# Splitting the score and maximum products of an attention stage into two matmuls of 64 weight columns

## What is computed

```
h = 8 heads of size 8, scale = 64 ** -0.5, n = 1056 rows, 8 samples
q, k, v = split(x @ w_qkv + b_qkv)
dots = einsum('bhid,bhjd->bhij', q, k) * scale
attn = softmax(dots, axis=-1)
out  = einsum('bhij,bhjd->bhid', attn, v)
```

## Time and profile before

| | |
|---|---|
| three runs | 2658.01, 2625.93, 2634.01 us; median 2634.01 us |
| profiled execution | 2648.98 us, its span 2647.2 us |
| mean granted TensorE clock | 0.86 of full speed |
| TensorE, VectorE, ScalarE busy | 81%, 50%, 43% of the span |
| attention stage | from 275.6 us (first maximum product) to 1234.8 us (last weighing) |

### The profile page before, as it was taken

One profiled execution on the slowest core, in us unless ns is written; L12 is line 12 of the kernel. 1 busy time (PEld: TensorE's weight loads), 2 busy tenths in 40 slices (PEclk: granted clock), 3 DMA queues, 4 the chain that ended last, 5 costly groups with the idle time before them and its releaser, 6 DMA issues. The chain is left out here.

```text
span 2647.2 us, 40358 instructions
## 1 busy us (share of the span) xinstructions
PE 2134.6 (81%) x14306; PEld 962.7 (36%) x14306; DVE 1323.2 (50%) x3515; ACT 1139.9 (43%) x2082; POOL 210.5 (8%) x238
## 2 busy tenths in 40 slices
PE   8975788888888888886758999970755998599999
PEld 4134122222222222211544544430324996345454
DVE  0036867777677777740124443437876443333331
ACT  0012066666666666664114454430521331254544
POOL 0021000000000000000000000003310133100000
PEclk9976589999899989987558999995876997699999
DMA  6825402121221212001110000000000000000000
GB/s 108 149 80 180 86 21 42 22 44 23 45 39 36 40 27 41 14 10 42 66 57 1 1 1 1 1 2 2 0 0 3 1 2 1 22 5 9 5 9 9
DMA packets 60311, 82.61 MB, mean 31 GB/s; under 512 B 26555, under 2 KB 45396, under 8 KB 57068
## 3 DMA queue, kind: packets, MB, share of 16 engines
q1 hardware_dynamic: 57036, 71.60, 12.6%
q0 software_dynamic: 3104, 8.72, 0.9%
HBM read 53.16 MB, written 27.14 MB: 30 GB/s over the span
## 5 line engine op out<-in xcount | busy, mean ns | idle before, releaser
L532 ACT ACTIVATE b_prob<-b_p_s 128x512 f32<-128x512 f32 x1104 | 590.2, 594 | 361.1 <-PE b_p_s L661 316.8
L546 DVE TENSOR_REDUCE b_m<-b_p_m 128x1 f32<-128x1024 f32 x512 | 602.4, 1219 | 215.7 <-PE b_p_m L608 214.7
L661 PE MATMUL b_p_s<-b_q,b_k 51*128 51x512 bf16 x1024 | 365.5, 420 | 120.1 <-DVE b_m L546 97.3
L608 PE MATMUL b_p_m<-b_k,b_q 48*128 48x512 bf16 x1024 | 374.7, 430 | 46.6 <-DMA b_k<-qk_scr 25.5
L688 PE MATMUL b_p_o<-b_prob,b_v 128*32 128x512 f32 x2304 | 340.9, 667 | 0.0
L661 PEld LDWEIGHTS b_p_s<-b_q,b_k 51*128 51x128 bf16 x1024 | 82.9, 96 | 509.1 <-DVE b_m L546 256.9
L1124 ACT ACTIVATE d_hidden<-d_p_z 128x704 f32<-128x704 f32 x192 | 135.5, 755 | 145.1 <-PE d_p_z L1028 144.8
L1124 ACT ACTIVATE n_hidden<-n_p_z 128x704 f32<-128x704 f32 x192 | 135.2, 755 | 127.8 <-PE n_p_z L1028 127.8
L1242 DVE TENSOR_TENSOR d_xg<-d_xd,d_p_c 128x352 f32<-128x352 f32 x192 | 91.3, 517 | 181.2 <-PE d_p_c L1017 181.2
L1242 DVE TENSOR_TENSOR n_xg<-n_xd,n_p_c 128x352 f32<-128x352 f32 x96 | 49.9, 520 | 203.4 <-PE n_p_c L1017 203.4
L1028 PE MATMUL d_p_z<-d_xg,d_w 64*128 64x352 f32 x768 | 144.0, 494 | 0.0
(11 more groups left out here) (317 smaller groups left out, 2584.2 us busy)
## 6 DMA issues: line engine op xcount, KB each, us to landing
xt<-in_x SPq DMA_DIRECT2D x16, 1024.0 KB, 11.7
v_scr<-a_vw SPq DMA_DIRECT2D x8, 1152.0 KB, 4.8
b_v<-v_scr SPq DMA_DIRECT2D x8, 1152.0 KB, 12.2
c_sums<-sum_scr SPq DMA_DIRECT2D x8, 1056.0 KB, 5.8
sum_scr<-b_sums POOLq DMA_DIRECT2D x32, 256.0 KB, 2.3
qk_scr<-a_qk_part SPq DMA_DIRECT2D x24, 264.0 KB, 2.9
b_q<-qk_scr SPq DMA_DIRECT2D x96, 66.0 KB
b_k<-qk_scr SPq DMA_DIRECT2D x16, 198.0 KB
```

Of the source, the lines that this page charges most:

```text
L532: nc.scalar.activation(prob[:, U % PR_RING, 0:w], p_s[:, U % S_RING, 0:w], ACT.Exp, scale=float(D) ** -0.5).then_inc(exp_done, 1)
L546: nc.vector.tensor_reduce(m3[:, x, 0:1], p_m[:, s, :, :].rearrange("p k n -> p (k n)"), axis=AX.X, op=ALU.max).then_inc(rows_free, 1)
L608: last = nc.tensor.matmul(out[:, k, :], q_st[s][r, i, t * P:t * P + P], k_st[s][r, i, k * WIDE:k * WIDE + WIDE], start=True, stop=True)
L661: last = nc.tensor.matmul(out, k_st[s][r, q, jt * P:jt * P + P], q_st[s][r, q, a * WIDE:a * WIDE + WIDE], start=True, stop=True)
```

## The change

Each of the 64 maximum products and 64 score products of a quad (L608 and L661) becomes two matmuls with 64 weight columns each. The first writes partitions 0 to 63 of the same PSUM bank, the second partitions 64 to 127. Both read the same moving operand. The semaphore is raised by the second. Waits, buffers, the order of the work and every other matmul stay as they are.

```diff
                     if x < FULL_ROWS:
                         i, t = divmod(x, FULL)
                         for k in range(2):
-                            last = nc.tensor.matmul(out[:, k, :], q_st[s][r, i, t * P:t * P + P], k_st[s][r, i, k * WIDE:k * WIDE + WIDE],
-                                                    start=True, stop=True)
+                            for e in range(0, P, 64):
+                                last = nc.tensor.matmul(out[e:e + 64, k, :], q_st[s][r, i, t * P + e:t * P + e + 64], k_st[s][r, i, k * WIDE:k * WIDE + WIDE],
+                                                        start=True, stop=True)
                             if k == 1:
                                 last.then_inc(rows_full, 1)
...
                 if a < 2 and jt < FULL:
-                    last = nc.tensor.matmul(out, k_st[s][r, q, jt * P:jt * P + P], q_st[s][r, q, a * WIDE:a * WIDE + WIDE], start=True, stop=True)
+                    for e in range(0, P, 64):
+                        last = nc.tensor.matmul(out[e:e + 64, :], k_st[s][r, q, jt * P + e:jt * P + e + 64], q_st[s][r, q, a * WIDE:a * WIDE + WIDE],
+                                                start=True, stop=True)
```

## The result

| | before | changed |
|---|---|---|
| median of four runs | 2630.58 us | 2835.23 us |
| lowest and highest | 2625.93 to 2658.01 | 2822.17 to 2846.65 |
| span of the profiled execution | 2647.2 us | 2820.4 us |
| mean granted clock over the span | 0.86 | 0.80 |

The ratio is 1.0747, 95% interval 1.0669 to 1.0826. The forecast of 2670 us and its range to 2735 us were wrong.

What follows compares the result with a forecast made beforehand. The prediction took the attention stage's loop of reduction, pair start, weighing and completing pair as the bound. Switches of 23 and 3 us plus starts of 10 us made 36 us on 2634, so 2670 us, range 2620 to 2735.

Steps and rivals of the forecast that it cites:

- The loop through the weighing: Attention stage: reduction, pair start, weighing and completing pair bound each group, 3.04 us by sum against 3.05 in the timeline.
- A round of four quadrants: Divided score and maximum products: four matmuls run at once in 0.22 us, like today's pair, so no gain.
- Switches around L619: Small maximum products: each shape change costs 0.10 us and the overlap, 1.54 us a quad, 23 us in 15 quads.
- Starts of divided products: Bursts behind a wait or a weighing: 0.02 us for each of 480 starts, 10 us, bounds 0 and 24.
- The page's load rule: Starts: without fast load, 53 ns for 64 columns against 27, making this term 18 us and the sum 44 us.
- The sum of 36 us: Whole kernel: 23 us and 3 us for switches plus 10 us for starts, bounds 0 and about 75.
- the added gaps brought a second fall: Rival on TensorE's granted clock: a second fall in each quad adds 61 us, giving 2731 us; chance 0.025.
- the serial stretch: Near a quad's end, maximum products share the scores' rows and run singly, 0.22 us apart; 18 of 64 score products.
- The halves one after another: Rival in the divided pairs: a pair holds TensorE for 0.44 us, adding 205 us, about 2840 us; chance 0.05.

Runs made afterwards that it cites:

- new order: Kernel before, undivided, with maximum products 15 pieces ahead instead of 16 and extra pieces after units 32 and 49 (two) instead of 22, 45, 68: 2540.74 us, ratio 0.9606.

## Why the prediction failed

- **What bounds the kernel: right.** The loop through the weighing was confirmed by breaking it: 96 us from a new order alone. In quads with one fall of 3.4 us each, where the clock is the same, a quad takes 49.6 us instead of 55.4.
- **A round of four quadrants takes as long as today's pair: right**, 0.22 to 0.24 us. There was no gain.
- **Switches around L619, 23 us: right in place and size.** Two scores and two pieces take 1.26 us as forecast. VectorE's idle time before that reduction, in a quad whose clock stays up, is 2.53 us, where 2.7 was said and before had 1.2.
- **Starts of divided products, 10 us: somewhat low**, 0.9 us a quad or 14 us in the new order with every product divided, inside the bounds of 0 and 24. That the whole of 36 us was met by 35 is thus in part luck: this term was too small and the switches were too large. What is left of the 2.3 us a quad is 1.4, an estimate across the two orders, instead of 26 / 15 = 1.7. The minimum of a 64-column load is 102 ns, between the 88 and 132 of the earlier trace rows.
- **The page's load rule: too high.** The Trainium skill says that column tiling turns off the fast weight load ("TensorEngine Tiling (Array Packing)", restrictions) and gives columns / 1.2 ns for a load ("TensorE: Matmul & The Clock Gate", LDWEIGHTS). The estimate from both was 26 ns more than now; the trace has 10.
- **The clock: here it failed.** The sum of 36 us put nothing for it; it stood as the rival in which "the added gaps brought a second fall", at 2731 us and a chance of 0.025. A second fall at the switches is what happened, and it cost 138 us where the sum had 0 and the rival 61. The rival's price was taken from one fall that the kernel already had, 13 us long, 4 us a quad. (That one was among the longest: they last 3.4 to 13.7 us, 8 on average, and 3 x 1.31 x 15 is 59.) The second fall lasts 51 to 55 us, through the serial stretch and the quad's turn, and comes in 8 of 14 passages. Why the clock does not come back there sooner is not shown; without a fall ahead the same stretches run at 1.00 in the quad of 57.72 us, but for 3.4 us. And its chance was taken too low: I priced the switches by their own length, 1.5 us a quad, and did not ask what a stretch does to the clock in which one product runs where two ran. The trace of before already had a hint: the fall at the turn of each quad, and the low clock in the last quad, where scores run alone.
- **The halves one after another** would have given 2840 us, the measured time within its error. It is refuted all the same by the starts, 0.01 us apart. A time that fits says little on its mechanism.

The Trainium skill, "TensorE: Matmul & The Clock Gate", section "Why this matters for your kernels", puts drops in the middle of a kernel down to idle gaps between bursts of matmuls. The trace has small gaps ahead of the fall: TensorE is busy for 1.07 of the 2.00 us from 786 to 788, and its longest wait there is 0.93 us. But the kernel before waits just as long at this place, 0.92 us, and keeps its clock, and so does the kernel with every product divided. And in the last quad of the new order the clock stays down with TensorE busy for 64.04 of 64.88 us. Idle gaps alone do not explain the falls.

Shown is this, in the order that the kernel has: small products of another width than their neighbours bring the long falls (in the changed kernel, and with only the small ones divided), and equal widths take them away (every product divided).

Open: what exactly in such a stretch makes the clock fall, and why only in some quads with the same instructions. The small products in one piece gave falls of 27 us at seven of 14 passages where no width changes, and none at all with two switches and no partner beside them; four pieces with eight switches gave 51 to 55 us at eight. Products one after another are not enough either: the stretch of the earlier trace rows runs at the higher clock. Switches with the overlap kept could not be made.

## What to carry to other kernels

Before an edit of TensorE's matmuls, list what runs beside what: a product of another column width does not overlap even in the opposite row half, and a switch costs 0.1 us. Then look at the granted clock stretch by stretch, and do not price thin work by its own length: 1.5 us of switches cost a quad 16 us here (73.55 against 57.72) where the clock fell with them. If one width has to be divided, divide its neighbours too, and if a stretch has an empty row half, filling it with work that nobody reads may be cheaper than leaving it empty, as it was in the last quad.

## What the runs showed of the hardware

- Column halves in both row halves, four matmuls of 64 x 512, run at once: started within 0.01 us, a round of 0.22 to 0.24 us.
- Matmuls of 64 and of 128 weight columns in opposite row halves are serialized: 0.55 us from start to start of products of 512 columns at 1.2 GHz, 0.29 to 0.34 us between a divided score and eight products of 32 columns, where the clock was 2.4 GHz for the most part.
- A 16-bit load of 64 weight columns takes 102 ns at the least, one of 128 columns 91 to 92 ns.
- TensorE at 99% busy can stay at the lower clock for a whole quad (0.55 over 64.88 us) and run at 1.00 when 64 products are added in the other row half (44.08 us).
- The same instructions can run with and without a long fall of the clock: quads of 57.72 and 73.55 us in the changed kernel, of 55.90 and 70.43 us in the kernel before with the small products in one piece.
